# Rows of the next stage made at the end of each stage, and attention's substitution moved one slot back, in a one-core transformer kernel

## What is computed

```python
x = x + 0.5 * ffn(layernorm(x))            # gate/up/down, hidden 768, silu
x = x + attention(layernorm(x))            # gated delta rule, 16 heads of 16, chunks of 64
x = x + 0.5 * ffn(layernorm(x))            # the same weights
x = x + 0.5 * binary(layernorm(x))         # +-1 weights, scale, bias, clip
x = x + state_space(layernorm(x))          # 128 complex modes, as a convolution
x = x + 0.5 * binary(layernorm(x))
```

```python
P = where(strict, (k_beta @ k.T) * L, 0)   # L from cumulated decays
Ainv = (I + P)(I + P^2)(I + P^4)...        # the inverse of a unit triangular matrix
v, k_cumdecay = Ainv @ v, Ainv @ (k_beta * exp(g))
# then a scan over the chunks with a 16x16 state per head
```

## Time and profile before

| | us |
|---|---|
| median of 3 runs | 1389.07 (1383.85 to 1390.11) |
| the profiled execution's own time | 1379.97 |
| its span, first to last instruction | 1378.2 |
| gates stage, 175.1 to 233.8 | 58.7 |
| delta stage, 233.8 to 967.5 | 733.7 |
| ffn stage (run 1), 967.5 to 1125.0 | 157.5 |
| PE, DVE, POOL, ACT busy | 1120.9, 956.3, 687.6, 578.6 |

### The profile page before, as it was taken

One profiled execution on the slowest core, in us unless ns is written; L12 is line 12 of the kernel. 1 busy time (PEld: TensorE's weight loads), 2 busy tenths in 40 slices (PEclk: granted clock), 3 DMA queues, 4 the chain that ended last, 5 costly groups with the idle time before them and its releaser, 6 DMA issues. The chain is left out here.

```text
span 1378.2 us, 42692 instructions
## 1 busy us (share of the span) xinstructions
PE 1120.9 (81%) x17226; PEld 800.5 (58%) x17226; DVE 956.3 (69%) x2654; ACT 578.6 (42%) x1449; POOL 687.6 (50%) x1446
## 2 busy tenths in 40 slices
PE   3999956657788887888897888766899979699968
PEld 3888722324556565555565555555688867345546
DVE  4777543387788878787788888763466645699963
ACT  3333153314455555555555555444433335210142
POOL 3666402544567656555576566333566536620045
PEclk9999987968999999998999999788799999899979
DMA  8000010112232221232222332310000003666002
GB/s 209 2 1 1 1 52 8 31 20 52 64 64 57 64 49 32 58 64 56 53 32 54 64 64 57 64 34 3 1 1 1 1 16 82 167 178 183 2 22 101
DMA packets 192740, 71.22 MB, mean 52 GB/s; under 512 B 139296, under 2 KB 187808, under 8 KB 192544
## 3 DMA queue, kind: packets, MB, share of 16 engines
q1 hardware_dynamic: 190944, 65.87, 20.6%
q10 hardware_dynamic: 1600, 2.62, 0.6%
HBM read 43.03 MB, written 21.23 MB: 47 GB/s over the span
## 5 line engine op out<-in xcount | busy, mean ns | idle before, releaser
L1679 DVE TENSOR_TENSOR delta_PR<-delta_PR,delta_tmp 128x30 f32<-128x30 f32 (+14 forms) x480 | 178.1, 371 | 11.5
L1677 DVE TENSOR_TENSOR delta_tmp<-delta_PR 128x30 f32<-128x30 f32 (+14 forms) x480 | 172.1, 358 | 9.2
L1545 ACT ACTIVATE delta_wide<-delta_S 32x128 f32<-32x128 f32 x256 | 78.6, 307 | 115.7 <-POOL delta_S L1824 61.7
L1334 PE MATMUL psum<-delta_T,delta_pad 128*32 128x128 f32 x2048 | 77.1, 310 | 21.3 <-DMA delta_T<-inverse_scratch 21.3
L518 POOL TENSOR_TENSOR ffn_H<-ffn_hid,ffn_H 128x512 fp32r<-128x512 f32 x48 | 61.6, 1289 | 56.2 <-DVE ffn_H L480 56.2
L518 POOL TENSOR_TENSOR first_H<-first_hid,first_H 128x512 fp32r<-128x512 f32 x48 | 61.6, 1288 | 53.7 <-DVE first_H L480 53.7
L1261 PE MATMUL psum<-both_w_in,delta_xT_t 128*128 128x512 f32 x128 | 80.0, 757 | 9.3 <-DVE delta_Kn L1633 7.8
L1347 PE MATMUL psum<-consts,delta_UT 128*32 128x128 f32 x512 | 49.2, 315 | 38.6 <-DVE delta_Bm L1687 36.6
L1334 PEld LDWEIGHTS psum<-delta_T,delta_pad 128*32 128x32 f32 x2048 | 66.0, 126 | 25.0 <-DMA delta_T<-inverse_scratch 23.3
L1312 PE MATMUL psum<-delta_MV,delta_KbT 32*32 32x128 f32 x2048 | 38.6, 286 | 37.3 <-ACT delta_UT L1520 20.7
L1528 ACT ACTIVATE delta_WT<-psum,consts 128x256 f32<-128x256 f32 x128 | 50.2, 475 | 43.6 <-PE psum L1334 43.0
(11 more groups left out here) (286 smaller groups left out, 3059.3 us busy)
## 6 DMA issues: line engine op xcount, KB each, us to landing
within_scratch<-delta_PT SPq DMA_DIRECT2D x128, 64.0 KB, 2.0
delta_PR<-within_scratch SPq DMA_DIRECT2D x16, 512.0 KB, 4.4
inverse_scratch<-delta_PR SPq DMA_DIRECT2D x16, 512.0 KB, 5.3
delta_T<-inverse_scratch SPq DMA_DIRECT2D x128, 64.0 KB, 2.4
space_T<-taps_scratch SPq DMA_DIRECT2D x8, 1024.0 KB, 6.1
X<-taps_scratch SPq DMA_DIRECT2D x8, 1024.0 KB, 9.0
X<-in_x SPq DMA_DIRECT2D x32, 128.0 KB, 10.2
late_X<-X SPq DMA_DIRECT2D x64, 64.0 KB, 2.0
```

What stands on the lines that cost most here:

```text
L1334: i = pe.matmul(bank[3][SUB * c:SUB * c + SUB, (2 * w + g) * P:(2 * w + g + 1) * P], M.pad[:, from_c:from_c + SUB], M.T[t % 2][:, h * P:(h ...
L1545: i = a.activation(states(M.wide[half])[rows, :, SUB * c:SUB * c + SUB], states(X)[rows, :, :], ACT.Copy)
L1677: i = v.tensor_tensor(t3, column.to_broadcast([P, j, n_after]), row.to_broadcast([P, j, n_after]), ALU.mult)
L1679: i = v.tensor_tensor(after, after, t3, ALU.add)
```

## The change

Five things, in the order of the stages:

1. SP issues the six loads of `w_in` at the end of the first stage's own loads (`start_sync`), not in gates. The memory of the first stage now lies within the region that is shared by gates and delta, so that `w_in` is free to be written.
2. ACT makes the next stage's first rows at the end of a stage: blocks 0 and 1 of gates at the end of first, all four tiles of each; block 0 of the second ffn at the end of delta; blocks 0 and 1 of binary at the end of ffn run 1. New helpers `scaled_rows` and `block_rows` do it, `S.f_new` says when the factors are there. POOL makes the second ffn's factors of blocks 0 and 1 in slots 37 and 38 of delta.
3. In gates DVE makes its rows of a block in front of a piece of the powers' work where it was behind it. PE's two steps for the taps and DVE's `taps_keep` go to the end; the reciprocal that gives `beta` and the scaling of `w_out` go behind `adec`.
4. In delta the substitution starts one slot later (even slot 2m+4), and apply, scan and output follow: lags 5, 6, 7, 8, and one slot more, n = -1 to 40. `pair_in(m)` stays in slot 2m+2. `pair_back(m)` goes to odd slots, 2m+5, where `pair_in` is not.
5. Rings grow by one for it: `gate` 9, `QgT` 7.

```diff
@@ start_sync
+    for name, o, c in (("Wb", QKVG, NH), ("Wa", QKVG + NH, NH), ("Wq", 0, DM), ("Wk", DM, DM), ("Wv", 2 * DM, DM), ("Wg", 3 * DM, DM)):
+        e.dma_start(M.w_in[:, :, o:o + c], rows_of(io[name])).then_inc(S.w_in, 16)
@@ ffn_scalar
     def rows(b):
+        if run == 1 and b == 0:
+            return
...
     ffn_order(gate_up, rows, turn, nothing)
+    for b in range(2):
+        a.wait_ge(S.f_new, blocks + b + 1)
+        if run == 0:
+            if b == 0:
+                a.wait_ge(S.xt_ps, 2 * NBLK)
+            a.wait_ge(S.up_mm, MH * (NBLK - 1))
+            block_rows(a, B, B.X, B.gates_xn[b], b).then_inc(S.a_xn, 1)
+        else:
+            block_rows(a, B, B.X, B.binary_xn[b], b).then_inc(S.b_xn, 1)
@@ ffn_gpsimd
-    if run == 1:
-        for b in range(2):
-            first_factors(g, own, B, S, run, b)
...
-        row_factors(g, own, B, B.MV, BLK * b, BLK * b + BLK)
+        row_factors(g, own, B, B.MV, BLK * b, BLK * b + BLK).then_inc(S.f_new, 1)
+def scaled_rows(a, B, X, dst, t):
+    return a.activation(dst, X[:, t, :], ACT.Identity, bias=B.shift[:, t:t + 1], scale=B.rstd[:, t:t + 1])
+
+def block_rows(a, B, X, dst, b):
+    for j in range(BLK):
+        i = scaled_rows(a, B, X, dst[:, j * DM:(j + 1) * DM], BLK * b + j)
+    return i
@@ gates_tensor
         if b == 5:
             turn_logits(0)
-            taps_turn_powers(pe, B, S)
-        if b == 6:
-            taps_products(pe, B, S)
     turn_logits(1)
+    taps_turn_powers(pe, B, S)
+    taps_products(pe, B, S)
@@ gates_vector
+    norm(2)
+    taps_angle(v, own, B, M, S)
+    norm(3)
+    norm(4)
+    taps_first_powers(v, own, B, M, S)
+    norm(5)
+    norm(6)
+    taps_last_powers(v, own, B, M, S)
+    norm(7)
+    taps_weights(v, own, B, M, S)
...
                     bcast_mid(M.A_row, NT), ALU.mult).then_inc(S.a_decay, 1)
+    v.reciprocal(M.beta, w0)
+    v.wait_ge(S.wo_in, 16)
+    v.tensor_scalar(M.w_out, M.w_out, M.nw_col, 0.5, ALU.mult, ALU.mult)
+    taps_keep(v, own, B, M, S)
     v.wait_ge(S.taps_out, 16)
@@ delta
-LAG_FORM, LAG_PAD, LAG_APPLY, LAG_SCAN, LAG_OUT = 1, 4, 5, 6, 7
+LAG_FORM, LAG_PAD, LAG_APPLY, LAG_SCAN, LAG_OUT = 1, 5, 6, 7, 8
@@ delta_sync
         if n % 2 == 0:
             if 0 <= (n - 2) // 2 < NT // 2:
                 pair_in((n - 2) // 2)
-            if 0 <= (n - 4) // 2 < NT // 2:
-                pair_back((n - 4) // 2)
+        elif 0 <= (n - 5) // 2 < NT // 2:
+            pair_back((n - 5) // 2)
@@ delta_scalar, at its end
+    a.wait_ge(S.f_rstd, NBLK + 1)
+    a.wait_ge(S.p_qk, NT)
+    a.wait_ge(S.p_vg, NT)
+    block_rows(a, B, B.X, B.ffn_xn, 0).then_inc(S.xn, 1)
@@ delta_vector, solve
-        m = (n - 3) // 2
+        m = (n - 4) // 2
...
-            k += 0 if n % 2 else HALF_SOLVE
+            k += HALF_SOLVE if n % 2 else 0
@@ delta_gpsimd, at the end of a slot
+        if n in (SLOTS - 4, SLOTS - 3):
+            first_factors(g, own, B, S, 1, n - (SLOTS - 4))
```

More of the change, by code:

```diff
@@ L187, in build @@
         late.close()
+        B.gates_xn, B.ffn_xn, B.binary_xn = made["gates"].xn, made["ffn"].xn, made["binary"].xn
         def phase_end(eng, n):
@@ L437, in rows @@
             a.wait_ge(S.xt_ps, 2 * (blocks + b))
[L438 to L441, removed]
+        block_rows(a, B, B.X, M.xn, b).then_inc(S.xn, 1)
     def turn(b):
@@ L611, in binary_memory @@
 def binary_memory(M, take):
+    M.Y = [take(f"Y{i}", 2 * DM) for i in range(4)]
     M.xn = [take(f"xn{i}", BLK * DM) for i in range(2)]
     M.XT = [[take(f"XT{s}{k}", 512) for k in range(KD)] for s in range(3)]
-    M.Y = [take(f"Y{i}", 2 * DM) for i in range(4)]
 def binary_tensor(pe, B, M, S, run):
@@ L663, in norm @@
             a.wait_ge(S.b_rstd, b + 1)
[L664 to L667, removed]
+        block_rows(a, B, X, M.xn[b % 2], b).then_inc(S.b_xn, 1)
     def keep(b):
@@ L674, in keep @@
             a.activation(M.XT[b % 3][k], B.bank[4 + k][:], ACT.Copy).then_inc(S.b_xt, 1)
-    norm(0)
-    norm(1)
+    if run == 1:
+        norm(0)
+        norm(1)
     for b in range(NBLK):
@@ L946, in gates_memory @@
 def gates_memory(M, take):
+    M.xn = [take(f"xn{i}", BLK * DM) for i in range(2)]
     M.vec = take("vec", 2 * NH + 1)
@@ L1058, in gates_scalar @@
             keep_logits(0)
-        if b == 6:
-            taps_keep_powers(a, B, S)
     keep_logits(1)
@@ L1084, in gates_vector, with norm @@
     bank, seq = B.bank, own.seq
-    for b in range(NBLK):
-        if b >= 2:
-            v.wait_ge(S.a_xt_ps, 2 * (b - 1))
+    def norm(b):
+        v.wait_ge(S.a_xt_ps, 2 * (b - 1))
         for j in range(2, BLK):
             i = normalize(v, B, M.xn[b % 2][:, j * DM:(j + 1) * DM], B.X, B.MV, BLK * b + j)
[L1090 to L1096, removed]
-        if b == 4:
-            taps_weights(v, own, B, M, S)
-    taps_keep(v, own, B, M, S)
+        i.then_inc(S.a_xn2, 1)
+    norm(2)
[8 more added lines that the diff above has]
+    taps_weights(v, own, B, M, S)
     w0, w1, w2 = M.wk
@@ L1109, in gates_vector @@
     seq(v.tensor_scalar(w0, w0, 1.0, None, ALU.add))
-    v.reciprocal(M.beta, w0)
-    v.wait_ge(S.wo_in, 16)
-    v.tensor_scalar(M.w_out, M.w_out, M.nw_col, 0.5, ALU.mult, ALU.mult)
     v.wait_ge(S.a_exp1, 1)
@@ L1160, in delta_memory @@
     M.Kn, M.Qn, M.Kb, M.Qg = (take(n, DM) for n in ("Kn", "Qn", "Kb", "Qg"))
-    M.VK, M.Kd, M.gate = some("VK", 6, 512), some("Kd", 7, DM), some("gate", 8, DM)
+    M.VK, M.Kd, M.gate = some("VK", 6, 512), some("Kd", 7, DM), some("gate", 9, DM)
     M.DU, M.E, M.KbT, M.MV = take("DU", 512), take("E", 512), take("KbT", DM), take("MV", 1024)
-    M.QgT, M.AT, M.PT = some("QgT", 6, DM), some("AT", 6, 512), take("PT", 512)
+    M.QgT, M.AT, M.PT = some("QgT", 7, DM), some("AT", 6, 512), take("PT", 512)
     M.PR, M.tmp = some("PR", 2, 1024), take("tmp", 256)
@@ L1468, in tanh_g @@
         a.wait_ge(S.p_vg, t + 1)
-        if t >= 8:
-            a.wait_ge(S.o_gate, t - 7)
-        a.activation(M.gate[t % 8], bank[5][:, DM:], ACT.Tanh, scale=0.5).then_inc(S.p_tanh, 1)
+        if t >= 9:
+            a.wait_ge(S.o_gate, t - 8)
+        a.activation(M.gate[t % 9], bank[5][:, DM:], ACT.Tanh, scale=0.5).then_inc(S.p_tanh, 1)
     def exp_decays(t):
@@ L1496, in keep_qg @@
         a.wait_ge(S.f_kb_ps, t + 1)
-        if t >= 6:
-            a.wait_ge(S.s_o, t - 5)
-        a.activation(M.QgT[t % 6], bank[2][:, DM:], ACT.Copy).then_inc(S.f_qgt, 1)
+        if t >= 7:
+            a.wait_ge(S.s_o, t - 6)
+        a.activation(M.QgT[t % 7], bank[2][:, DM:], ACT.Copy).then_inc(S.f_qgt, 1)
     def spread_vk(t):
@@ L1614, in keep_gate @@
     def keep_gate(t):
-        gate = M.gate[t % 8]
+        gate = M.gate[t % 9]
         v.wait_ge(S.p_v, t + 1)
@@ L1837, in gate_o @@
         g.wait_ge(S.o_mul, t + 1)
-        g.tensor_tensor(M.o_sb, M.o_sb, M.gate[t % 8], ALU.mult).then_inc(S.o_gate, 1)
+        g.tensor_tensor(M.o_sb, M.o_sb, M.gate[t % 9], ALU.mult).then_inc(S.o_gate, 1)
     for n in range(-1, SLOTS):
```

22 lines of the change are left out of this document (9 added, 13 removed).

## The result

The changed kernel takes 1340.08 us (median of 4 runs, 1325.63 to 1341.41) against 1389.48 of the kernel before on the same chip (4 runs, 1383.85 to 1390.11). The ratio is 0.963, with a 95% interval of 0.956 to 0.970: 49 us less. The prediction was 1343.

A forecast was written before the change was run, and what follows sets the result against it. Waits bound delta and gates; in delta, the wait for P and the return of T run side by side. Terms -30 + 1.3 - 13 - 4.2 = -46 took profiled 1379.97 to 1334, plus 9 for the median: 1343, range 1320 to 1372.

The forecast's parts named there:

- likeliest case: In delta, each start slot wins 1 to 3 us: 1343 us, own range 1328 to 1358, chance 0.63.
- Start slots: In delta, a shorter return of T makes 15 start slots 2.0 us shorter each: 30 us less.
- The extra slot: In delta, slot 3 without substitution adds 4.3 us, one more slot without forming saves 3: net +1.3.
- Gates: Gates stage: weights -6, rows -5, ln no longer waiting -2.4, work behind adec +0.4; -13 us (-8 to -16).
- The term for the weights: In gates, w_in and both blocks' rows are there when the stage begins, so PE starts earlier: -6 us.
- the order of the rows: In gates, DVE's rows no longer stand behind the powers: 5 us won (0 to 8).
- Second ffn: Second ffn's start: factors and rows are done before the stage, so 4.2 us less; up to 2 could come back.
- Binary: Binary's first product waits for weights DVE makes only at 1130.30, so earlier rows win 0; were rows the bound, -2.
- The return isn't shortened: Rival in delta: the copy's time stays or T's loads take the saving; 0.45 us per start slot, 1366; chance 0.20.
- DVE bounds: Rival in delta: T comes early enough in most start slots, 3.6 us each won, 54 in all, 1319; chance 0.07.
- Lower clock: Rival in delta: PE's longer wait leaves apply at 1.2 GHz, 2.6 us more per start slot, 1412; chance 0.05.
- Neither: Rival: delta gives nothing and pays for more of a slot, gates gives half; within 7 us of before; chance 0.05.

The follow-up runs named there:

- run 0: Not a follow-up run: the first binary stage within a kernel's execution; 60.3 us in the kernel before, 62.1 in the changed kernel.
- experiment 3: Changed kernel with an added 512 KB read of P into an unused tile, issued right before each copy back: 1378.49 us, ratio 0.992.
- experiment 11: Kernel with only the seams changed, plus lags 5 to 8, so T has a slot of slack but the wait for P stays: 1366.57 us, ratio 0.985.
- experiment 1: Kernel before with the delta changes alone; gates, ffn and binary untouched: 1361.07 us, ratio 0.981.
- experiment 4: Changed kernel with apply, scan and output one slot later still (lags 6 to 9), rings one larger: 1329.92 us, ratio 0.958.
- experiment 10: Changed kernel with lags 6 to 9 and rings one larger, run again beside the changed kernel on one chip: 1323.49 us, ratio 0.954.
- experiment 6: Changed kernel with binary's rows of blocks 0 and 1 made at that stage's own start again: 1342.98 us (2 runs), ratio 0.969.
- experiment 7: Changed kernel with beta's reciprocal and the scaling of w_out back in front of ln's input: 1346.04 us (2 runs), ratio 0.971.
- experiment 9: The changed kernel run again, unaltered: 1339.40 us, ratio 0.965 against the kernel before.
- experiment 12: Changed kernel with the loads of w_in at the start of gates again: 1343.35 us (2 runs), ratio 0.968.
- experiment 2: Changed kernel with delta put back, larger rings kept, so the seams alone are changed: 1369.52 us, ratio 0.987.
- experiment 8: Kernel before with only SP's order changed, the copy back issued in front of the read of P: 1384.78 us, ratio 0.999.

## Why the prediction was right

The forecast, 1343 with its likeliest case (start slots winning 1 to 3 us), was right in its mechanism: measured 1340. That the total is this near is in part luck, since two of its terms were off by about as much in opposite directions. A stage's length also varies from one execution to the next, so I set all profiles beside each other, each where its code of that stage is that of one kernel or the other (us):

| stage | code of before | changed code | difference of means | forecast |
|---|---|---|---|---|
| gates | 58.8, 60.6, 60.4 | 41.9 to 44.6 (nine) | -16.7 | -13 |
| delta | 733.6, 736.0 | 705.7 to 712.6 (six) | -25.9 | -28.7 |
| second ffn | 157.6, 158.2, 159.1 | 153.7 to 154.9 (eleven) | -3.9 | -4.2 |
| binary run 0 | 60.3, 63.6, 62.2, 61.9 | 61.7 to 63.4 (ten) | +0.4 | 0 |

The four together give -46.1 for a forecast -46: delta won some 3 us less than forecast, gates some 4 more.

- **What bounds the kernel**: two latencies side by side, of which `pair_in`'s is the longer wait but not the only one. Start slots take 23.0 us before, 23.1 with the wait for P gone but a read beside the copy (experiment 3), 22.2 with slack for T but the wait for P kept (experiment 11), and 20.5 to 21.1 with both gone. In time the one or the other wins nothing that is clear of noise, both together 29 (experiment 1).
- **Start slots (-30)**. The forecast's working holds part by part up to `apply`: the copy 3.56 for 3.65, the first load 3.28 for 3.4, `apply` 7.72 for 7.8. `own_heads` came at 10.39, even before the 11.0, for a reason that the forecast did not have: `apply` itself ran faster, 2.19 for 2.66, being at the upper clock in 12 of 14 start slots where in 11 of 14 before it was wholly or partly at the lower. Of the 2.8 won at `own_heads` only 2.2 are left in the slot, since I had left "the rest of a start slot" at 9.9 and it became 10.45, as `keep_within` now waits longer for PE. The first twelve second slots grew by 0.3, most of it before `own_heads` in three of them. A pair of slots went from 41.1 to 39.0, the 39 that was forecast. The case in which start slots win 3.6 each did not come here, though with a slot of slack for T they win 3.0 and 3.9 (20.0 and 19.1 us in experiments 4 and 10).
- **The extra slot (+1.3)**. Slot 3's own part is as read: 264.02 - 253.46 = 10.56 us between the starts of these two rows for the forecast 10.6, and slot 4 begins without a wait.

```profile
253.46 0.75 DVE L1660 TENSOR_TENSOR delta_AT<-psum,delta_E 128x256 f32<-128x256 f32 x2
...
264.02 0.75 DVE L1660 TENSOR_TENSOR delta_AT<-psum,delta_E 128x256 f32<-128x256 f32 x2
264.74 0.09 DVE L1686 MEMSET delta_PR<- 128x32 f32 x1
```

- **Delta in all**: forecast -28.7; -25.1 between the two profiles, and -21 to -28 with the five other profiles of this delta (experiments 1, 6, 7, 9, 12). Between the two profiles it divides so: up to the first marked slot +3.8 and slot 33 without a tile to form -3.0, together +0.8 for the extra slot; 14 start slots -30.3; twelve second slots +3.9; the end +0.6. What the sum had left out is the longer second slots.
- **Gates (-13)**: -15.0 between the two profiles, -16.7 between the means. The term for the weights was mis-sized: 6 forecast, 3.5 to 4.3 by experiment 12, depending on the profile it is compared with. The reciprocal's 2.4 less 0.4 is borne out (+2.5 to +3.0 when undone, in one profile). By subtraction, some 9 to 10 us belong to the order of the rows, where I took 5 and allowed up to 8; no run tried that part alone, so this split is not shown. At the stage's end DVE takes 7.6 us from the end of `adec` for its reciprocal, taps and store where I summed 7.2.
- **Second ffn (-4.2)**: its transposes start 0.1 us after the stage does, for 4.2 before; the stage is 3.2 shorter between the two profiles and 3.9 between the means.
- **Binary (0)**: the spread of the stage is 3 us with the code of before alone, so 0 cannot be told from 1 or 2 there.
- **The rivals.** *The return isn't shortened*: experiment 3 is that case made on purpose, and it gives 1378; in the changed kernel the copy alone is as short as in slot 35 of before. That slot's late `own_heads` (12.7), the argument for the rival, repeats in slot 36 (12.9), where `apply` takes 3.64 us after a wait of 4.57: it is a matter of the last slots, not of the return. *DVE bounds*: no, in the slots DVE now waits for PE, as the rows show. *Lower clock*: PE's wait in front of `apply` did get longer, 1.41 us for 0.89, as this rival had it, but `apply` ran at the upper clock more often than before, not less. From the slot's start to `apply` the granted clock was 0.97 on average for 0.91, so PE came to its wait at the upper level more often; what keeps it there no run tried by itself. After waits of 2.3 to 4.6 us `apply` was at the lower clock in slots 32, 34 and 36, though not in slot 20, after 3.2 us. *Neither*: ruled out by experiments 1 and 2.

The ring order that the prediction quoted from the Trainium skill ("DMA: Bandwidth & Descriptors", section Queues, rings and completion order) now has its rows: behind a 512 KB read the same copy takes 5.1 us (experiment 3), in front of it 3.2 (experiment 8). By that rule all of the forecast's 1.65 us was the read's price, and this the runs bear out, at 1.8 (5.34 to 3.56).

## What to carry to other kernels

When the longest wait is one of two latencies that start together, price the other before removing the first; here each alone won nothing clear of noise and both 29 us. A transfer that delays whoever stands behind it was not cured by swapping the order; moving it to a slot where nothing is behind it was. Once the return had a whole slot of slack, PE no longer waited for it: 10 to 16 us more were to be had by one more step of lag (experiments 4 and 10). And a difference between two profiles of a stage says little until it is known how much the stage varies where its code is the same: gates by 2.7 us, delta by 7 here.

## What the runs showed of the hardware

- One 512 KB read issued 0.4 us ahead of a 512 KB copy on the same queue adds 1.6 to 1.8 us to it (3.56 without it; 5.14 with it in experiment 3, 5.34 in the kernel before). Issued behind it, the read adds nothing to the copy (3.24), but 2.2 us to the time from the small loads that follow until `apply` starts (6.53 for 4.36). I had expected a shared cost for both.
- The read's harm was larger than the copy's delay: start slots 2.3 us longer in experiment 3 than in the changed kernel for 1.6 of the copy. The rest is the read's issue (0.4 us) and `apply` at the lower clock more often (0.5 us on average).
- The 64 matmuls of `apply` take 1.95 us at the upper clock and 3.64 at the lower. Waits of 1.7 and 1.9 us in front of them ended in the one and in the other, so from a wait of this length alone the clock could not be told here.
- The same six loads of `w_in` hold SP about 1 us each when they are issued behind the 32 loads of x in the first stage (first two rows), and 0.4 to 0.5 each at the start of gates (last two, from experiment 12):

```profile
20.74 1.05 SPq L262 DMA_DIRECT2D both_w_in<-in_Wb  x1
21.84 0.93 SPq L262 DMA_DIRECT2D both_w_in<-in_Wa  x1
```

```profile
174.40 0.39 SPq L975 DMA_DIRECT2D both_w_in<-in_Wb  x1
174.83 0.47 SPq L975 DMA_DIRECT2D both_w_in<-in_Wa  x1
```

- Executions of one and the same kernel spread by up to 16 us (1325.63 to 1341.41), more than several of the effects here. Several runs on one chip, and the stage read from several profiles, told them apart where they could be told apart.
